# Two products for the running sum, and 128 rows for two small spreads, in a decoder layer

## Time and profile before

| | |
|---|---|
| three executions | 2572.60, 2575.54, 2579.24 us, median 2575.54 |
| profiled execution | 2577.89 us, its span 2576.1 us |
| TensorE products busy | 2293.4 us (89%), 20736 records |
| weight loads busy | 1866.1 us (72%), beside the products |
| VectorE, ScalarE, GpSimd busy | 74%, 55%, 27% |
| chain that ended last | PE 47%, DVE 28%, ACT 10%, issue 10% |
| mean granted clock of TensorE | 0.974 |

### The profile page before, as it was taken

The page is one execution under the profiler, slowest core; times in us unless marked ns, Lnnn a source line. Parts: engine busy times, 40 slices in busy tenths (PEclk is TensorE's granted clock), DMA queues, the critical chain, the costliest instruction groups (busy, mean ns, idle before and its releaser), DMA issues.

```text
span 2576.1 us, 55768 instructions
## 1 busy us (share of the span) xinstructions
PE 2293.4 (89%) x20736; PEld 1866.1 (72%) x20736; DVE 1915.4 (74%) x4589; ACT 1424.4 (55%) x4586; POOL 702.4 (27%) x1065
## 2 busy tenths in 40 slices
PE   3879999999999999999999999999999999999964
PEld 3667777777777777777777777777777777777753
DVE  3568787778777777878777877777787877787753
ACT  3445655565655556565556565555656555656532
POOL 0123233222233222323222223322222322222321
PEclk9889999999999999999999999999999999999976
DMA  4010111111111111011111011111101111111111
GB/s 113 17 34 26 42 42 50 50 42 33 43 34 50 50 50 39 29 42 42 50 50 42 28 48 34 50 50 51 40 28 42 42 50 51 42 34 34 34 34 41
DMA packets 267474, 109.96 MB, mean 43 GB/s; under 512 B 215235, under 2 KB 248259, under 8 KB 267203
## 3 DMA queue, kind: packets, MB, share of 16 engines
q1 hardware_dynamic: 258498, 89.61, 14.0%
q10 hardware_dynamic: 8704, 16.78, 1.7%
HBM read 89.57 MB, written 16.78 MB: 41 GB/s over the span
## 4 chain that ended last, share of the span: by engine, by line
PE 47%; DVE 28%; ACT 10%; issue 10%; POOL 3%; SPq 1%; DMA 1%; POOLq 0%; DVEq 0%; ACTq 0%
PE ps_g L593 38%; PE ps_g L601 7%; ACT p_a L945 4%; DVE neg_max L1233 3%; PE ps_s L593 3%; DVE qk L1226 2%; DVE decay L1353 2%; DVE ctx_t L1384 2%; DVE x_tok L1289 2%; POOL qk_rot L1570 2%; DVE ctx_t L1382 2%; DVE ln_stat_b L1196 1%; DVE ln_stat_a L1196 1%; DVE f_max L1464 1%; ACT p_all L945 1%
## 5 line engine op out<-in xcount | busy, mean ns | idle before, releaser
L945 ACT ACTIVATE p_a<-ps_s,neg_max 128x128 f32<-128x128 f32 (+1 forms) x1024 | 415.2, 442 | 63.5 <-DVE neg_max L1233 63.5
L593 PE MATMUL ps_g<-x_t_hi,wqkv_hi 128*128 128x256 f32 x1024 | 304.5, 297 | 19.0 <-DVE p_t L1262 17.6
L593 PE MATMUL ps_g<-x_t_lo,wqkv_hi 128*128 128x256 f32 x1024 | 286.1, 279 | 0.0
L593 PE MATMUL ps_g<-x_t_hi,wqkv_lo 128*128 128x256 f32 x1024 | 285.8, 279 | 0.0
L1233 DVE TENSOR_REDUCE neg_max<-ps_s 128x2 f32<-128x256 f32 (+1 forms) x512 | 257.4, 544 | 5.2 <-PE ps_s L593 5.2
L1657 POOL TENSOR_SCALAR p_all<-p_all,f_rec,g_bc 128x256 f32<-128x256 f32 x256 | 152.2, 607 | 362.0 <-DVE f_rec L1472 362.0
L1570 POOL TENSOR_TENSOR qk_rot<-qk_rot,const 128x512 f32<-128x512 f32 x128 | 164.5, 1285 | 296.9 <-DVE qk_rot L1219 296.8
L945 ACT ACTIVATION_READ_ACCUMULATOR p_a<-ps_s,neg_max 128x1 f32 x1024 | 234.5, 229 | 0.0
L996 ACT COPY p_t<-ps_g 128x384 f32<-128x384 f32 x256 | 119.2, 479 | 196.7 <-PE ps_g L601 194.2
L601 PE MATMUL ps_g<-const,p_a 128*128 128x128 f32 x1536 | 223.4, 284 | 4.2 <-ACT p_t L996 1.4
L593 PEld LDWEIGHTS ps_g<-x_t_hi,wqkv_hi 128*128 128x128 f32 x1024 | 194.8, 190 | 36.0 <-DVE p_t L1262 23.7
(11 more groups left out here) (202 smaller groups left out, 6281.5 us busy)
## 6 DMA issues: line engine op xcount, KB each, us to landing
x_tok<-in_x SPq DMA_DIRECT2D x32, 512.0 KB, 3.6
ctx<-in_ctx SPq DMA_DIRECT2D x64, 256.0 KB, 3.5
p_all<-in_L_ffn_Wq SPq DMA_DIRECT2D x128, 128.0 KB, 2.6
pt_all<-in_L_ffn_Wk SPq DMA_DIRECT2D x128, 128.0 KB, 3.1
y_out<-in_L_ffn_Wv SPq DMA_DIRECT2D x128, 128.0 KB, 3.2
out<-y_out ACTq DMA_DIRECT2D x32, 512.0 KB, 2.8
x<-in_L_attn_Wqkv SPq DMA_DIRECT2D x2, 512.0 KB, 7.9
p_all<-in_L_attn_Wqkv SPq DMA_DIRECT2D x1, 512.0 KB, 4.4
```

Of the source, the lines that this page charges most:

```text
L593: return nc.tensor.matmul(o, l, r, start=first, stop=last)
L945: return nc.scalar.activation(o, i, f, **kw)
```

## The change

The running sum is made by one product of all eight columns with `upto`, and one of `one` with block 0 that adds to the last four columns. `m_parts`, `minus_pick` and `r_g` have 128 partitions instead of 36, 36 and 1; the rows between hold zeros, from one wider and one new fill on GpSimd at the start, and so the products "decay" and "g" contract over 128 rows. (`minus_pick` repeats its pattern every 32 rows; rows of `m_parts` from 36 on are zero.)

```diff
-    m_parts = sb("m_parts", [LO_AT + HX, T], F32R)
-    minus_pick = sb("minus_pick", [LO_AT + HX, HX], F32R)
+    m_parts = sb("m_parts", [P, T], F32R)
+    minus_pick = sb("minus_pick", [P, HX], F32R)
...
-    r_g = sb("r_g", [1, 2 * KF])
+    r_g = sb("r_g", [P, 2 * KF])
...
-            mm(o[:, 0:HX], upto, log_f[:, 0, :], True, True)
-            mm(o[:, HX:2 * HX], c["one"].to_broadcast([P, P]), log_f[:, 0, :], True, False)
-            mm(o[:, HX:2 * HX], upto, log_f[:, 1, :], False, True).then_inc(filled.sem)
+            mm(o[:, 0:2 * HX], upto, log_f.rearrange("p t h -> p (t h)"), True, False)
+            mm(o[:, HX:2 * HX], c["one"].to_broadcast([P, P]), log_f[:, 0, :], False, True).then_inc(filled.sem)
...
-                    done = mm(o[:, j * T:(j + 1) * T], minus_pick[:, 2 * hp + j:2 * hp + j + 1].to_broadcast([LO_AT + HX, P]), m_parts, True, True)
+                    done = mm(o[:, j * T:(j + 1) * T], minus_pick[:, 2 * hp + j:2 * hp + j + 1].to_broadcast([P, P]), m_parts, True, True)
...
-            mm(o[:, 0:2 * KF], c["one"][0:1].to_broadcast([1, P]), r_g, True, True).then_inc(filled.sem)
+            mm(o[:, 0:2 * KF], c["one"].to_broadcast([P, P]), r_g, True, True).then_inc(filled.sem)
...
-            v.tensor_tensor(m_parts[LO_AT:], m_row, m_parts[0:HX].bitcast(F32), ALU.subtract).then_inc(m_split.sem)
+            v.tensor_tensor(m_parts[LO_AT:LO_AT + HX], m_row, m_parts[0:HX].bitcast(F32), ALU.subtract).then_inc(m_split.sem)
...
-        v.tensor_copy(minus_pick, c["minus_pick"][0:LO_AT + HX]).then_inc(tables_ready.sem)
+        v.tensor_copy(minus_pick, c["minus_pick"]).then_inc(tables_ready.sem)
...
-        g.tensor_scalar(m_parts, const[0:LO_AT + HX, 0:T], 0.0, None, ALU.mult).then_inc(half_ready.sem)
-        pool.wait_ge(half_ready.sem, 5)
+        g.tensor_scalar(m_parts, const[:, 0:T], 0.0, None, ALU.mult).then_inc(half_ready.sem)
+        g.memset(r_g, 0.0).then_inc(half_ready.sem)
+        pool.wait_ge(half_ready.sem, 6)
```

More of the change, by code:

```diff
@@ L933, in tensor @@
         pe.wait_ge(setup_loaded.sem, SETUP)
-        pe.wait_ge(half_ready.sem, 5)
+        pe.wait_ge(half_ready.sem, 6)
         pe.wait_ge(stage_split.sem, PIECES)
@@ L1184, in scalar @@
         act.wait_ge(tables_ready.sem, 4)
-        act.wait_ge(half_ready.sem, 5)
+        act.wait_ge(half_ready.sem, 6)
         act.wait_ge(stage_split.sem, PIECES)
@@ L1432, in stage_c @@
             dve.wait_ge(*routed(b, 9))
-            v.tensor_scalar(r_g[:, 0:KF], r_eg, r_s[:, 7:8], None, ALU.mult).then_inc(routed.sem)
+            v.tensor_scalar(r_g[0:1, 0:KF], r_eg, r_s[:, 7:8], None, ALU.mult).then_inc(routed.sem)
             dve.wait_ge(*routed(b, 10))
-            v.scalar_tensor_tensor(r_g[:, KF:], r_g[:, 0:KF], float(DF) ** -0.5, r_g[:, 0:KF], ALU.mult, ALU.mult).then_inc(routed.sem)
+            v.scalar_tensor_tensor(r_g[0:1, KF:], r_g[0:1, 0:KF], float(DF) ** -0.5, r_g[0:1, 0:KF], ALU.mult, ALU.mult).then_inc(routed.sem)
             yield
```

## The result

Nine runs of the changed kernel have a median of 2567.08 us (2562.87 to 2570.26). Nine of the kernel before, run in between, have 2577.19 us (2572.6 to 2580.2). The ratio is 0.9963, with a 95% interval of 0.9954 to 0.9972: by this ratio 9.5 us faster, between 7.2 and 11.9. The prediction said 8.6 us off and 2566.9 us. The total is right; the way to it is not, as the traces show. The profiled execution took 2565.48 us.

What follows compares the result with a forecast made beforehand. It took the chain of waits to bound the kernel, with VectorE idle for TensorE's decay and rotary products after `m_parts`. Decay joint 6.4 + sum 1.9 + last pass's joint 0.3 = 8.6 us off, giving 2566.9 us; range 2560 to 2575.

Steps and rivals of the forecast that it cites:

- The sum's third product, steady passes: Running sum on TensorE: dropping its third product saves 0.22 us a pass, which goes into existing waits.
- The sum's third product, the seven passes at half clock: Seven passes without a wait for `m_parts`: the 0.22 us saved in the sum counts, 7 x 0.22 = 1.5 us.
- there TensorE runs through: In those seven passes TensorE works from the sum to the rotary block without idle time, so 1.5 us is saved.
- C: Rival: shorter passes make the half-clock stretches fall elsewhere; five fewer save 4.2 us, giving 2562.7 us; chance 0.13.
- D: Rival: less TensorE work around the sum drops the clock in nearly every pass, 24 more falls, 2586.8 us; chance 0.08.
- The joint between decay and rotary products: TensorE after `m_parts`: the 0.20 us lost between products of 36 and 128 rows goes, 32 x 0.20 = 6.4 us.
- The pause inside the decay group: Among the four decay products: a step 0.10 us too long, expected to stay because it follows an idle wait.
- Rival B: The pause inside the decay group goes too, 32 x 0.10 = 3.2 us more, giving 2563.7 us; chance 0.12.
- A: Rival: rows don't matter, the long joint before the rotary products stays; only 1.9 us saved, 2573.6 us; chance 0.15.
- The gate spread: Gate product `r_g` at 128 rows: new joint after `m_col`, covered by the 0.26 us idle before the decay products.
- my two ends: Bounds for the new joint between `m_col` and `r_g`: 0.11 us (32 to 128 rows) and 0.20 us (36 to 128).
- The end: Last pass, all at half clock: 0.4 us saved in the sum, about 0.3 more from its joint.

Runs made afterwards that it cites:

- the first four experiments: Sum edit alone 2568.52 us; both spreads alone 2574.49 us; changed kernel with decay spread back at 36 rows 2570.49 us; with gate spread back at one row 2570.84 us.
- the next two: Changed kernel plus one full-width product behind the running sum: 2566.82 us; kernel before with the sum's first product done twice: 2582.08 us.

## Why the prediction was right or wrong

**The sum's third product, steady passes: right.** Covered, 0.22 us went into the wait for `a_col`.

**The sum's third product, the seven passes at half clock: wrong.** I counted 7 x 0.22 = 1.5 us, as if these passes stayed what they were. They are gone, 7 x 0.85 = 6 us in the profiled pair. That this edit does it, the first four experiments and the next two show: the traces with the edit have no stretch in the steady passes, those without it have four to ten. The step that failed is "there TensorE runs through": I took the stretches as given and priced the removed work inside them, though the earlier trace rows shows the half clock right behind the wait and the tiny products. My rivals C and D did ask whether their number would change. C was near in number (five fewer) but gave shorter passes as the reason, and the kernel with the sum edit alone keeps its passes at 75.90 us and has no stretch. D had the sign backwards: it counted the tiny products as work that holds the clock. With a third of them gone the full-width products come 0.22 us sooner and the clock holds; with a third more of them there are ten stretches.

**The joint between decay and rotary products: right in mechanism, half in size.** The 0.20 us is gone, 31 times. The term was 6.4 us and measured 31 x 0.09 = 2.8: the sum left out that the 24 products behind would change their own pace, which takes back 0.11 us of the 0.20. A steady pass takes 75.78 us, where I gave 75.66. The kernel with the spreads alone gives 3.4 us (1.0 to 5.7). Of a change of tiling mode the Trainium skill ("TensorEngine Tiling (Array Packing)", section "Key Properties") says that the engine drains there; by that rule the trace agrees, with 0.20 us at the joint and none without it.

**The pause inside the decay group: right to leave it in.** Four products still fill 0.73 us. Rival B is out by this, and A by the joint that is gone.

**The gate spread: right.** Its new joint takes 0.10 us of the wait before the decay products, the lower of my two ends, and nothing of the time.

**The end.** I had 0.7 us for the last pass. From the last sum on the changed kernel takes 110.7 us and the kernel before 111.7 and 112.0 in its two profiles; the kernels with two sum products and no filler 109.8 to 110.7, one of them 111.6.

**The total.** 1.9 + 6.4 + 0.3 was predicted. The traces give 2.8 for the spreads, some 3.5 to 6 for the stretches (four or seven of them at 0.85) and 1 at the end, 7 to 10, with 9.5 measured. Two errors of opposite sign, -3.6 and +2 to +4.5, cancelled. The total was right by luck, then, not by the steps.

**Left open.** What chooses between 113.3 and 117.8 ns. And which passes lose the clock, where any do: in the profiled run before, five of the six gaps between stretches are 228.7 us, three passes and one loss, and the last 749 us of steady passes have none. So something beside the pass's own work, the same in each, decides it.

## What to carry to other kernels

Look at the granted clock pass by pass, not as a mean of 0.97: seven stretches at half clock cost 6 us, twice what the joints were worth (2.8 us). Where TensorE waits and then does tiny products before its next full block, look for the clock behind it. There one product of 0.22 us, itself covered by a wait, went with losses of 0.85 to 1.0 us in some passes. Fewer tiny products kept the clock up. In the last passes, where TensorE has little work, full-width products into a free bank, placed ahead of a wait that would be idle anyway, did so, and that was worth 11 us of 110 in the trace. And a removed pause ahead of a long run of products can be partly paid back by the run itself: time the run's pace before and after, not the pause alone.

## What the runs showed of the hardware that I had not expected

- Tiny f32 products (8 columns, about 0.11 us from start to start) kept TensorE busy for 86 of 110 us and left the granted clock at 0.70; with full-width ones in the same places it was busy for 77 of 104 us and the granted clock was 0.84.
- A block of F32R products of 128 rows and 256 columns runs at 113.3 or at 117.8 ns from start to start at full clock, for the whole block, with the same operands and in the same place of the program. Behind a change from 36 to 128 rows it was 113.3 in 30 of 31 passes (28 to 31 over five traces), without the change 117.8 in 31 of 31 (21 to 31 over nine), and the order of the operands made no difference.
- A change of row height cost TensorE 0.20 us from 36 to 128 rows and 0.10 from 4 to 128; the height itself cost next to nothing (weight loads of 36 and 128 rows 188 and 192 ns, four decay products 0.72 and 0.73 us).
